# A graph layer with a mixture of experts: one landing wait more ahead of each group's scatters, none in the gathers of the last groups

## The reference, cut to what matters

```python
x = x + gnn(layernorm(x), adj, ...)        # adj @ x, W1, rms norm, silu, W2
u = layernorm(x)
gate_logits = u @ gate_w + gate_b
topk_vals, topk_idx = top_k(gate_logits, 2)
topk_w = softmax(topk_vals)
h = relu(einsum('bsh,ehf->bsef', u, w1) + b1)
expert_out = einsum('bsef,efh->bseh', h, w2) + b2
moe = sum(topk_w * take(expert_out, topk_idx))
y = u + moe
x = x + layernorm(y) * gamma + beta
```

## Time and profile before

| what | us |
|---|---|
| timed runs, median of 3 | 1091.09 |
| lowest and highest of them | 1085.10, 1094.84 |
| the profiled execution's own time | 1082.17 |
| its span, first to last instruction | 1080.3 |
| TensorE matmul busy in it | 804.2 |
| VectorE busy | 632.8 |
| ScalarE busy | 529.9 |
| GpSimd busy | 508.1 |

### The profile page before, as it was taken

How to read it: one execution, slowest core, us unless ns; L and a number is a source line. 1 busy time by engine, 2 the same in 40 slices (tenths; PEclk the granted TensorE clock), 3 DMA queues, 4 the chain that set the end, 5 groups by cost and what they waited for, 6 DMA issues and landing times. The chain is left out here.

```text
span 1080.3 us, 19075 instructions
## 1 busy us (share of the span) xinstructions
PE 804.2 (74%) x4717; PEld 600.9 (56%) x4718; DVE 632.8 (59%) x2292; ACT 529.9 (49%) x1123; POOL 508.1 (47%) x540
## 2 busy tenths in 40 slices
PE   5998888888988888875769888898888888830000
PEld 4686666566666566654557666676666666620000
DVE  3786677666676667772555554666665556532223
ACT  3797667676876667764113232444433434321111
POOL 2025555554554455565400545554555545455553
PEclk9999889889988889995789999999988999875555
DMA  4553444344433431113355656666766666731112
GB/s 146 175 201 122 148 146 128 128 139 144 149 127 123 133 128 58 59 65 97 91 169 148 174 160 174 178 190 183 194 170 189 181 183 197 195 99 56 54 57 66
DMA packets 141531, 149.20 MB, mean 138 GB/s; under 512 B 18835, under 2 KB 113059, under 8 KB 141222
## 3 DMA queue, kind: packets, MB, share of 16 engines
q1 hardware_dynamic: 122614, 111.13, 34.6%
q0 software_dynamic: 16384, 34.11, 10.8%
q10 hardware_dynamic: 2480, 3.40, 0.9%
HBM read 83.02 MB, written 65.55 MB: 138 GB/s over the span
## 5 line engine op out<-in xcount | busy, mean ns | idle before, releaser
L508 POOL DMA_INDIRECT dispatched<-rows,slot_i x256 | 251.9, 984 | 273.5 <-issue 197.6
L532 POOL DMA_INDIRECT work<-results,place x184 | 178.2, 969 | 224.3 <-issue 75.9
L867 ACT ACTIVATE hid<-bank,wts 128x256 f32<-128x256 f32 x286 | 118.8, 470 | 286.7 <-PE bank L704 172.9
L704 PE MATMUL bank<-tut,wts 128*128 128x256 f32 x572 | 163.1, 411 | 35.0 <-DVE tut L1275 26.0
L1297 DVE SCALAR_TENSOR_TENSOR tout<-bank,gate,tin 128x128 f32<-128x128 f32 x274 | 83.8, 346 | 162.2 <-PE bank L719 102.6
L719 PE MATMUL bank<-w_all,hid 128*128 x1144 | 174.7, 298 | 0.0
L719 PEld LDWEIGHTS bank<-w_all,hid 128*128 128x128 f32 x1144 | 146.7, 201 | 18.4 <-issue 2.6
L564 PEld LDWEIGHTS bank<-w_sb,work 128*128 128x128 f32 x1024 | 125.9, 194 | 33.8 <-issue 30.4
L564 PE MATMUL bank<-w_sb,work 128*128 128x128 f32 x1024 | 133.0, 279 | 14.0 <-issue 12.1
L558 PE MATMUL bank<-agg,w_sb 128*128 128x512 f32 x256 | 137.8, 665 | 0.0
L704 PEld LDWEIGHTS bank<-tut,wts 128*128 128x128 f32 x572 | 104.7, 204 | 51.0 <-DVE tut L1275 26.7
(11 more groups left out here) (195 smaller groups left out, 1073.9 us busy)
## 6 DMA issues: line engine op xcount, KB each, us to landing
tin<-dispatched SPq DMA_DIRECT2D x143, 132.0 KB
wts<-in_w_exp SPq DMA_DIRECT2D x143, 129.0 KB
results<-tout SPq DMA_DIRECT2D x26, 704.0 KB
results<-tout SPq DMA_DIRECT2D x137, 128.0 KB
xs<-in_x SPq DMA_DIRECT2D x32, 256.0 KB
adj_sb<-in_adj_t SPq DMA_DIRECT2D x32, 256.0 KB
rms_b<-r_row SPq DMA_DIRECT2D x32, 256.0 KB
out<-agg SPq DMA_DIRECT2D x32, 256.0 KB
```

The source lines that it names most:

```text
L508: nc.gpsimd.indirect_dma_start(dispatched, bass.IndirectOffsetOnAxis(slot_i[:, k, n:n + 1], 0), rows[:, k, n // TOPK, n % TOPK, :], None). ...
L532: nc.gpsimd.indirect_dma_start(moe_of(g)[:, n // TOPK, n % TOPK, :], None, results, bass.IndirectOffsetOnAxis(place[:, g, n:n + 1], 0)).th ...
L704: last = nc.tensor.matmul(hid_ps[n % 2][:, c * TILE:(c + 1) * TILE], wts[:, k, c * P:(c + 1) * P], tut[:, n % 2, :], start=True, stop=True)
L867: last = nc.scalar.activation(hid[:, n % 2, c, :], hid_ps[n % 2][:, c * TILE:(c + 1) * TILE], ACT.Relu, bias=wts[:, k, F + c:F + c + 1], s ...
```

## The change

Ahead of the scatters of every group but the first stands one more wait: all 8 scatters of the group before must have landed. In the gathers, the wait for the group before and the wait after the first four now hold for g < `MIXED` only, so for the groups 0 to 22. The groups 23 to 31 (nine groups, 72 gathers) keep their waits for `t_out`, `place_done` and `p_n`. No instruction that computes or moves data is added, removed or put elsewhere.

```diff
                     pool.wait_ge(slot_done, count(i, g + 1))
                     pool.wait_ge(tanh_done, count(i, g + 1))
+                    if g >= 1:
+                        pool.wait_ge(scattered[(g - 1) % RING], count(i, (g - 1) // RING + 1, 16 * GB * TOPK, 1))
                     pool.nop(nofuse=True)
...
-                if g >= 1:
+                if 1 <= g < MIXED:
                     pool.wait_ge(moe_in[(g - 1) % RINGM], 16 * GB * TOPK * ((g - 1) // RINGM + 1))
                 pool.nop(nofuse=True)
                 for n in range(GB * TOPK):
-                    if n and n % BURST == 0:
+                    if g < MIXED and n and n % BURST == 0:
                         pool.wait_ge(moe_in[g % RINGM], 16 * (GB * TOPK * (g // RINGM) + n))
                         pool.nop(nofuse=True)
```

## The result

The changed kernel took 1114.61 us (median of 4 runs, 1107.96 to 1118.72), beside 1090.35 us for the kernel before (4 runs, 1085.10 to 1094.84): ratio 1.0218, 95% interval 1.015 to 1.0287. It is slower by some 2%, where I had forecast 1053.6 and given "slower" 0.03. The profiled execution took 1115.53 us, its span is 1113.5. In the changed kernel every line from the scatters on has a number two higher (the scatter is L510, the gather L534).

The account below looks back on a forecast made before the run. The prediction took TensorE and its feeding to bound stage one, the tiles stage two, and POOL's gathers with landing waits the last some 120 us. Gathers -37.5 and scatters 0 from the 1091.09 median gave 1053.6 us, range 1044 to 1067.

Parts of the forecast that it names:

- Scatters: cost taken 0: Stage one: each head wait costs POOL 1.8 us, but idle time hides it, so 0 us is added.
- the upper bound: Scatters in stage one: if each of 31 head waits delayed everything, 31 x 1.8 = 56 us lost.
- A pair costs 3.6 more, which 4.10 covers: Scatters: two head waits per pair of groups add 3.6 us; POOL's smallest idle ahead of a pair, 4.10, absorbs it.
- Thinnest slack 1.8 us, at `rows`: End of stage one: ScalarE's `rows` of group 30 has 1.8 us before later scatters of group 27 delay it.
- Gathers: 37.5: Gather groups 23 to 31: dropping 18 landing waits, some 2.1 us each, saves 37.5 us.
- The tiles: cost 0: Gathers from group 23: the tiles are done in time for the earlier gathers, so `t_out` waits add 0.
- The buffers: cost 0: Last gather groups: `p_n` of nine groups earlier is ready in time, cost 0, with some 60 us of cover.
- Stage two by the tiles: Middle of the kernel: the tiles were taken as the limit that sets stage two's pace.
- Stage one pays: Rival: head waits reach ScalarE's ring wait at `rows`; 18 us slower, 1109; chance 0.03, plus 0.06 for a mild form.
- The limit on gathers in flight: Rival, last gathers: POOL must wait for room beyond four under way, pace stays 1.79 us, time 1091; chance 0.05.
- The stretch by VectorE: Rival, last nine groups: VectorE's two-tile additions lengthen gathers by 18.6 us, gain 18.9, time 1072; chance 0.06.
- the shut-out: Contrary rule, last gathers: each VectorE addition with two SBUF inputs would stop POOL for its whole length; trace bears it out little.

Follow-up runs that it names:

- e17: Kernel before plus only the wait at each scatter group's head, on kind one: 1129.35 us against 1087.37, ratio 1.0382.
- e11: Kernel before plus the scatters' head wait in groups 26 to 31 alone, on kind two: 1023.87 us against 1014.08, ratio 1.0109.
- e10: Changed kernel with SP's 26 transfers of zeros issued in stage one's first seven steps, on kind two: 1077.89 us against before's 1014.08, ratio 1.0624.
- e4: Kernel before, unchanged, run once more on kind two: 1021.62 us in its one run.
- e12: Kernel before without landing waits in scatters and in gathers of groups 0 to 22, on kind one: 1215.05 us against 1084.99, ratio 1.1164.
- e2: Kernel before with gathers of groups 23 to 31 free of landing waits, scatters unchanged, on kind two: 982.06 us against 1018.39, ratio 0.965.
- e16: Kernel before with gathers of groups 23 to 31 free of landing waits, scatters unchanged, on kind one: 1065.86 us against 1087.37, ratio 0.9792.
- e9: Kernel before without any landing wait in scatters or gathers of any group, on kind two: 848.37 us, ratio 0.8362.

## Why the prediction was wrong, step by step

- *"Scatters: cost taken 0."* This is the step that failed: the head waits alone cost 42 us on kind one (e17). The price for the new wait itself, 1.8, is nearly right: the 31 heads of the changed kernel idle 2.25 us on average, 1.95 over the bare gap; e11's six cost 9.8, 1.6 each, with an interval of 1.0 to 2.7. What was wrong was to price it alone, both in the 3.6 for a pair and in the upper bound. The old middle wait grew as well, from head to middle by 9.09 - 7.12 = 1.97 on average. Together that is 3.9 a group. The idle time that was to cover it was 2.58 ahead of a head on average, 2.3 over the bare gap, and all of it went; 3.9 less 2.3 is 1.6, and the heads moved from 14.57 to 16.21 apart, 1.64. Over 31 groups that is 51 us, and the last scatter ends 52 later. By this sum the 1.95 alone would have been covered.
- *Why the middle wait grew* is shown in part. From 0.5 us ahead of a head to 1.6 us behind the fourth scatter SP issues at most 512 KB in 20 of the groups 3 to 23 of the kernel before, and the middle idles 2.1 to 2.4 on average; in 17 of these groups of the changed kernel it issues 1.2 to 1.5 MB, and the middle idles 4.9 to 5.1. So the head wait shifts a group's scatters onto SP's transfers, and e10 shows that the zeros among them make the wait longer. Bytes alone don't settle it: in e4, with 1.0 to 1.2 MB in 19 of these groups, the middle idles 2.3 to 3.2.
- *"A pair costs 3.6 more, which 4.10 covers."* I took the idle time ahead of a pair for slack, without asking what made it. (It also holds the bare gap of 0.30, so the cover was 3.8.) The traces point to the eight scatters in a row: on kind one VectorE's `msv` waited 51.5 us in 11 waits, eight of which end 1.45 to 1.61 us behind such a run. With the head wait no run is longer than four, and these waits are gone. Heads stood 14.57 apart on kind one and 12.65 on kind two before, and with both waits 16.21 and 16.53: that fits the loss of 42 us on the one and 110 on the other. No run changes the length of the scatters' runs on kind one and nothing else, so this cause is argued; e12, with no landing wait in its scatters, bears it out.
- *"Thinnest slack 1.8 us, at `rows`."* The place was right. From group 4 on, in the changed kernel, `rows` starts some 1.5 us behind the end of the scatters of three groups before.
- *"Gathers: 37.5."* Right in size where TensorE's signals are on time: 36 us in e2. On kind one 21.5 (e16). In the changed kernel the last gather came 20.0 later than before: 38.3 from stage one, less 37.5, plus 7.49 and 10.04 of new waits and some 2 of slower gathers. The end behind it grew from 10.5 us to 23.6, since the late tiles had held up VectorE's groups too. The sum is 33 us between the two spans; the medians differ by 24.3, since the execution profiled before was 8 us faster than its median.
- *"The tiles: cost 0."* Failed on kind one, and "The buffers: cost 0" with it: group 29 waited 7.49 us for a tile and group 31, said to have 60 us of cover, 10.04 for a buffer. I had checked when the tiles would be done at before's pace, and not whether gathers without a pause could slow the tiles. (952 + 8 x 1.27 is 962.2 and not 962.6; nothing hangs on it.)
- *"Stage two by the tiles."* Wrong: by POOL's list (e9, on kind two). It cost the forecast nothing, but it hid by far the largest gain.
- *The rivals.* "Stage one pays" was the right one, with its place; it had 0.03 and a rule ("decides once the idle time is shorter than 3.6") whose own price was half of the true one. The limit on gathers in flight didn't show: the changed kernel has gathers 1.25 apart for six whole groups. The stretch by VectorE did show, but small. In e2 the last 72 gathers take 3.7 us more than 0.94 each, all of it in 29 that run beside VectorE's additions of two tiles (mean 1.06, longest 1.45); the other 43 take 0.94. The longest, with the addition beside it:

```profile
896.02 1.45 POOL L533 DMA_INDIRECT rows<-results,place  x1 [0.30 <-issue]
```

```profile
895.96 0.69 DVE L1351 TENSOR_TENSOR rows<-rows 128x512 f32<-128x512 f32 x1
```

The 3.7 us are a fifth of the 18.6 that this rival was given. Of the shut-out that the Trainium skill states in "SBUF — State Buffer", section "Who interferes with whom", the trace of e2 shows a part: gathers beside the additions are stretched, but by 0.12 us on average and 0.51 at the most, and not by an addition's whole 0.69. The little weight that it had was right.

Of the versions that were run on both kinds of chip, only e2's (e16's) beats both kernels on both: the middle wait of the scatters as before, the gathers of the last nine groups free. e9's is 16% faster on kind two, and was not run on kind one; e12, which has most of it, makes one expect it to be slower than before there.

## What to carry to other kernels

Before calling idle time slack, find what makes it: a gap that comes once per pattern may be the price of that pattern. Price an added wait together with the waits that are there already, since it moves them against the other queues' bursts; where eight transfers and two waits add up to the whole distance between groups, as they did here, suspect a bound, whatever the other engines' busy shares say. And measure on more than one chip before shipping a change that lengthens unbroken runs of software-queue DMAs.

## What was not expected of the hardware

- A landing wait has no fixed price. Behind four scatters of 1.26 us it idled 2.1 to 2.4 us in the kernel before on kind one, about 5 in the changed kernel with 1.2 to 1.5 MB of SP's transfers beside them, and 3.5 to 3.8 with the 704 KB of zeros moved away (e10).
- Two kinds of chip, 1085 to 1091 and 1014 to 1023 us for the same kernel. On the slower kind, engines that wait for TensorE go on late after its end while POOL issues indirect DMAs without a pause: 6.8 us behind eight of them in the kernel before, 24.7 in the unbroken gathers of the changed kernel; the longest such wait is 22.7 in e12 and 3.2 in e17, where a landing wait stands after every four. On the faster kind none occurs, even in e9. Why the kinds differ, and what carries the signal, no run tells.
